# A decoder layer on one Trainium2 core: three groups of fp32 products as split products, base rows through DRAM

## What is computed

```
x = x + attn(layernorm(x))        # 16 heads of 128, window 128, rotary, q and k normed, a sink logit
x = x + cross(layernorm(x), ctx)  # 16 heads of 32, causal; out = concat(heads) @ Wout.T
x = x + ffn(layernorm(x))

attn:  q = h @ wq_comp @ wq_up    # 512 -> 128 -> 2048
       ... softmax ...            # then 2048 -> (4 groups) -> 512
ffn:   h = rmsnorm(x); base = x   # residual inside the sublayer as well
       routed = top 4 of 32 experts, w1: 512 -> 2*256, w2: 256 -> 512, silu(g)*u
       shared = silu(h @ sg) * (h @ su) @ sd      # 512 -> 512 -> 512
       out = base + routed + shared
```

## Time and profile before

| | |
|---|---|
| median of three runs | 1190.68 us |
| the profiled execution, its own time | 1187.81 us |
| its span, first to last instruction | 1185.9 us |
| mean granted TensorE clock | 0.989 |
| TensorE (PE) busy | 1141.3 us, 96% |
| weight loads (PEld) | 901.9 us, 76% |
| VectorE (DVE) | 811.3 us, 68% |
| ScalarE (ACT) | 594.3 us, 50% |
| GpSimd (POOL) | 344.8 us, 29% |

### The profile page before, as it was taken

One profiled execution on the slowest core, in us unless ns is written; L12 is line 12 of the kernel. 1 busy time (PEld: TensorE's weight loads), 2 busy tenths in 40 slices (PEclk: granted clock), 3 DMA queues, 4 the chain that ended last, 5 costly groups with the idle time before them and its releaser, 6 DMA issues. The chain is left out here.

```text
span 1185.9 us, 21051 instructions
## 1 busy us (share of the span) xinstructions
PE 1141.3 (96%) x7761; PEld 901.9 (76%) x7762; DVE 811.3 (68%) x1392; ACT 594.3 (50%) x1404; POOL 344.8 (29%) x279
## 2 busy tenths in 40 slices
PE   6989999999999999999999989999999999999995
PEld 3457677777767777776777666887889999999994
DVE  1255797889789878978987886643266666666662
ACT  1334554565455446545544644421146666666662
POOL 0011103211311221131123112222046666666643
PEclk9999999999999999999999989999999999999998
DMA  8450000000000000000000005042089999999974
GB/s 279 143 175 19 1 9 10 14 16 2 16 14 9 9 14 16 8 10 14 9 9 16 14 10 204 9 163 80 28 293 264 258 261 280 269 274 271 271 148 54
DMA packets 62598, 117.59 MB, mean 99 GB/s; under 512 B 10932, under 2 KB 14564, under 8 KB 62388
## 3 DMA queue, kind: packets, MB, share of 16 engines
q1 hardware_dynamic: 44820, 82.46, 20.6%
q0 software_dynamic: 17728, 34.44, 14.6%
HBM read 93.55 MB, written 28.13 MB: 103 GB/s over the span
## 5 line engine op out<-in xcount | busy, mean ns | idle before, releaser
L1503 POOL TENSOR_TENSOR rall<-qkv_var,phalf 100x17 f32<-100x17 f32 x16 | 49.1, 3071 | 404.4 <-DVE qkv_var L1177 404.4
L391 PE MATMUL QS<-xh,wh 128*128 128x256 f32 x512 | 147.2, 288 | 0.0
L392 PE MATMUL QS<-xl,wh 128*128 128x256 f32 x512 | 144.8, 283 | 0.0
L393 PE MATMUL QS<-xh,wl 128*128 128x256 f32 x512 | 144.8, 283 | 0.0
L1581 POOL DMA_INDIRECT out_rows<-work,idx x64 | 106.1, 1658 | 101.3 <-DMA out_rows<-work,idx 47.1
L391 PE MATMUL W<-wch,oth 128*100 128x512 f32 x256 | 105.1, 410 | 0.0
L392 PE MATMUL W<-wcl,oth 128*100 128x512 f32 x256 | 100.6, 393 | 0.0
L393 PE MATMUL W<-wch,otl 128*100 128x512 f32 x256 | 100.4, 392 | 0.0
L392 PEld LDWEIGHTS QS<-xl,wh 128*128 128x128 f32 x512 | 98.2, 192 | 1.2
L391 PEld LDWEIGHTS QS<-xh,wh 128*128 128x128 f32 x512 | 98.0, 191 | 1.2
L393 PEld LDWEIGHTS QS<-xh,wl 128*128 128x128 f32 x512 | 98.1, 192 | 0.0
(11 more groups left out here) (225 smaller groups left out, 2863.3 us busy)
## 6 DMA issues: line engine op xcount, KB each, us to landing
raw<-in_w SPq DMA_DIRECT2D x24, 1024.0 KB
raw<-in_w SPq DMA_DIRECT2D x24, 512.0 KB
work<-in_w SPq DMA_DIRECT2D x8, 1024.0 KB
work<-in_w SPq DMA_DIRECT2D x8, 512.0 KB
hx_rows<-h3x SPq DMA_DIRECT2D x16, 212.5 KB
h_columns<-h3s SPq DMA_DIRECT2D x16, 200.0 KB, 1.9
h3T<-h_columns SPq DMA_DIRECT2D x4, 800.0 KB, 15.2
out_rows<-ytiles POOLq DMA_DIRECT2D x14, 200.0 KB, 2.5
```

Source lines behind the costliest of these rows:

```text
L391: mm(dst, ah, bh, start=start, stop=False)
L392: mm(dst, ah, bl, start=False, stop=False)
L393: return mm(dst, al, bh, start=False, stop=stop)
L1503: return nc.gpsimd.tensor_tensor(out=dst, in0=src, in1=phalf[:, 0:src.shape[1]], op=ALU.pow)
```

## The change

1. `queries` for sequences 2 to 15 and `cross_out` for all become split products. The weights are split once: ScalarE copies `w_uph` and `w_outh` in step 0, VectorE subtracts `w_upl` at the end of step 0 and `w_outl` in step 1. Per step ScalarE's copy of the compressed query now writes the high part `hqh`, and VectorE gets `queries_low` (128 x 100); ScalarE's copy of the cross values writes `oxh`, and VectorE gets `values_low` (128 x 400).
2. To make room, `resid` holds eight sequences' rows instead of sixteen. After the third norm SP stores the base rows of a sequence to DRAM (`row_out`) and in steps 2 to 9 loads the residual rows of the sequence eight later into the place (`row_in`). Before the shared network's sums it loads all base rows back (`base_back`), in tiles of 128 tokens.
3. The shared network's second layer goes over 13 tiles: three of 128 tokens in each group of 400, and one of the 16 tokens left in each of the four groups. ScalarE and VectorE copy and subtract these 16 columns apart (`lfh`, `lfl`) for each inner product.
4. `cross_out` in the loop writes QS's bank 3 instead of W's. TensorE's heads 12 and 13 of `project` move behind `cross_transposed`, head 14 behind `cross_values`; on VectorE `rotate_keys` moves behind `rotate`; on ScalarE the exponential of the router moves behind the copies of the cross probabilities. Some semaphores are merged.

```
+HELD = 8
+LEFT = QW % BLK
+WHOLE = 2
             def queries(c):
+                whole = isinstance(c, int) and c < WHOLE
                 pe.wait_ge(s.hqT, c + 1)
+                if not whole:
+                    pe.wait_ge(s.hq_low, c - WHOLE + 1)
+                    if isinstance(c, int) and c == WHOLE:
+                        pe.wait_ge(s.low, NH + 1)
                 for i in range(4):
-                    mm(qb[i][0:T, :], hqT[:, :], w_up[:, 512 * i:512 * (i + 1)], start=True, stop=True).then_inc(s.q_ps, 1)
+                    w = slice(512 * i, 512 * (i + 1))
+                    if whole:
+                        last = mm(qb[i][0:T, :], hqT[:, :], w_up[:, w], start=True, stop=True)
+                    else:
+                        last = split_product(qb[i][0:T, :], hqh[:, :], hql[:, :], w_uph[:, w], w_upl[:, w], True, True)
+                    last.then_inc(s.q_ps, 1)
...
-            def cross_out(b):
+            def cross_out(b, bank):
-                pe.wait_ge(s.oxT, b)
+                pe.wait_ge(s.ox_low, b)
...
                 for k in range(KC):
-                    last = mm(wb[3][0:T, :], oxT[:, T * k:T * (k + 1)], w_out[:, 512 * k:512 * (k + 1)],
-                              start=k == 0, stop=k == KC - 1)
+                    c, w = slice(T * k, T * (k + 1)), slice(512 * k, 512 * (k + 1))
+                    last = split_product(bank[0:T, :], oxh[:, c], oxl[:, c], w_outh[:, w], w_outl[:, w], k == 0, k == KC - 1)
...
             def row_out(c):   # SP
+                sp.wait_ge(s.ln3_base, c + 1)
+                sp.wait_ge(s.row_st, 48 + 16 * c)
+                sp.dma_start(dst, resid[0:T, slot]).then_inc(s.row_st, 16)
+            def row_in(c):
+                sp.wait_ge(s.row_st, 48 + 16 * (c + 1))
+                sp.wait_ge(s.ld_x, 16 * (c + 1))
+                sp.dma_start(rv[:, bass.ds(c, 1), :], xv[:, bass.ds(c + HELD, 1), :]).then_inc(s.ld_x, 16)
...
             sp.wait_ge(s.x2_ps, NB)
+            sp.wait_ge(s.ld_x, 16 * (HELD + 1))
+            sp.wait_ge(s.row_st, 48 + 16 * NB)
+            for g in range(4):
+                base_back(g)
+            for g in range(4):
+                at = QW * g + 3 * BLK
+                sp.dma_start(back_left[LEFT * g:LEFT * (g + 1), :], based[at:at + LEFT, :]).then_inc(s.ld_x, 16)
...
+            def queries_low(c):   # VectorE
+                dve.wait_ge(s.hqT, c + 1)
+                dve.wait_ge(s.q_ps, 4 * c)
+                tt(hql[:, :], wb[1][:, 0:T], hqh[:, :].bitcast(fp32), ALU.subtract).then_inc(s.hq_low, 1)
+            def values_low(b):
+                dve.wait_ge(s.oxT, b)
+                dve.wait_ge(s.x2_ps, b - 1)
+                tt(oxl[:, :], wb[1][:, 0:QW], oxh[:, :].bitcast(fp32), ALU.subtract).then_inc(s.ox_low, 1)
...
-            def shared_rows(g, some=range(4)):
+            def shared_rows(g, some=range(3)):
                 for t in some:
+                    u = 3 * g + t
+                    dve.wait_ge(s.sh_y_ps, u + 1)
+                    if 2 <= u <= 10:
+                        dve.wait_ge((s.sh_st0, s.sh_st1)[u % 2], 16 * (u // 2))
+                    if t == 0:
+                        dve.wait_ge(s.ld_x, 16 * (HELD + 9))
+                    tt(ytile[sum_at(u)], back[g][:, HID * t:HID * (t + 1)], wb[t][:, :], ALU.add).then_inc(s.sh_y, 1)
```

More of the change, by code:

```diff
@@ L324, in step @@
                     sp.dma_start(dst, h3x[:, :]).then_inc(s.hx_st, 16)
-            pipeline(sp, step)
+                if do.C:
+                    row_out(b - 2)
+                if swap:
+                    row_in(b - 2)
+            step(0)
+            step(1)
+            with sp.Fori(2, HELD + 2) as b:
+                step(b, True)
+            again[0] = 1
+            with sp.Fori(HELD + 2, NB - 1) as b:
+                step(b)
+            step(NB - 1)
             def load_columns(g, done):
@@ L607, in step @@
                     router(b - 2)
-                if do.A:
-                    project(b, range(12, 14))
                 if do.X:
@@ L617, in step @@
                 if do.A:
-                    project(b, range(14, 15))
+                    project(b, range(12, 14))
                 if do.X:
@@ L624, in step @@
                 if do.A:
-                    project(b, range(15, 16)).then_inc(s.x1_ps, 1)
+                    project(b, range(14, 16)).then_inc(s.x1_ps, 1)
                 if do.C:
                     if do.X:
-                        pe.wait_ge(s.oxT, b)
+                        pe.wait_ge(s.ox_low, b)
                     ranks(b - 2)
                 if do.X:
-                    cross_out(b)
+                    pe.wait_ge(s.pxT, 4 * b)
+                    cross_out(b, qb[3])
             join(range(0, 8))
@@ L730, in _ @@
             shared_outer(3)
+            left_outer()
             def inner(e, v):
@@ L824, in compressed @@
                 act.wait_ge(s.q_ps, 4 * c)
-                copy(hqT[:, :], banks[1][:, 0:T]).then_inc(s.hqT, 1)
+                whole = isinstance(c, int) and c < WHOLE
+                copy((hqT if whole else hqh)[:, :], banks[1][:, 0:T]).then_inc(s.hqT, 1)
                 act.wait_ge(s.kv_ps, c + 1)
@@ L1277, in step @@
                 if do.Q:
-                    if isinstance(b, int) and b < 2:
-                        dve.wait_ge(s.ld_x, 16 * (b + 1))
+                    if isinstance(b, int) and b == 0:
+                        dve.wait_ge(s.ld_x, 16)
+                    elif not isinstance(b, int) or b >= HELD - 1:
+                        dve.wait_ge(s.ld_x, 16 * (b + 1 - HELD) + 32 if again[0] or isinstance(b, int) else 16)
                     ln_stats(0, b + 1, s.ln1_stats, s.ln1_var)
@@ L1325, in step @@
                     rotate(b + 1)
+                if do.Q:
+                    rotate_keys(b + 1)
                 if do.X:
                     cross_normed(b)
+                if isinstance(b, int) and b == 1:
+                    out_weights_low()
                 if do.Q:
@@ L1362, in _ @@
             joined(range(13, 14))
-            pipeline(dve, step)
+            step(0)
+            step(1)
+            with dve.Fori(2, HELD - 1) as b:
+                step(b)
+            for b in range(HELD - 1, HELD + 2):
+                step(b)
+            again[0] = 1
+            with dve.Fori(HELD + 2, NB - 1) as b:
+                step(b)
+            step(NB - 1)
             def split_low(n):
```

206 lines of the change are left out of this document (132 added, 74 removed).

## The result

| | before | changed |
|---|---|---|
| median of 20 runs each, us | 1193.95 (1186.55 to 1211.33) | 1189.16 (1180.54 to 1203.72) |
| ratio, 95% interval | 1 | 0.9955 (0.9934 to 0.9975) |
| span of the profiled execution, us | 1185.9 | 1181.5 |
| granted clock | 0.989 | 0.984 |

The ratio leaves out the executions that took over 1.5% longer than the fastest of their kernel. By it the change gains 5.4 us, 0.45%; forecast were 13.9 and a median of 1176.8 us. Of the 12.4 us between that and the measured median, 3.3 are the kernel before itself: its median was 1190.68 us over the first three runs and is 1193.95 over 20. The two profiles differ by 4.4 us, and that difference is read stretch by stretch.

What follows compares the result with a forecast made beforehand. TensorE was taken to fill the 41.40 us step, VectorE's chain close behind. Loop -9.8, step 15 -0.8 and shared network -3.3 gave -13.9 from 1187.81: 1173.9, plus 2.9 for the median, 1176.8 us; range 1167 to 1188.

Steps and rivals of the forecast that it cites:

- Split products: TensorE's `queries` and `cross_out`: four split products take 2.80 us, saving 0.63 and 0.69, 1.32 us a step.
- The wait at `hql`: TensorE in front of `queries`: 0.78 us of the saving turns into waiting for VectorE's subtraction, taken as 0.25 us.
- The ring: Loop steps: TensorE and VectorE wait on each other, so a step goes from 41.40 to 40.65 us, gaining 0.75.
- Rival 1: Loop: TensorE keeps the bound and a step gives all 1.6 us; 11 us more gain, 1166 us; chance 0.10.
- rival 2: Loop: VectorE's added work costs 0.75 us more a step, so the loop gives 0; 1186.6 us; chance 0.24.
- Step 15: Last step: step 14's `cross_out` saving passes through, with the wait of `cross_values`: -0.8 us, bounds 0 to -1.0.
- Group 0: Shared network's first group: base rows and a store delay product 7 to about 804.8; +2.3 us, bounds 0 to +10.
- rival 4: Loop: the wait in front of `queries` lowers the clock each step, 22 us on top, 1199 us; chance 0.05.
- Rival 3: Shared network: base rows land 12 us later at half the load rate, 1189 us; chance 0.07.
- The experts: Experts' stretch behind the shared network: its own 300 us untouched, 0 forecast.

Runs made afterwards that it cites:

- e4: Changed kernel with `queries` plain in all steps, `cross_out` still split: median 1188.65 us, ratio 0.9962, step 40.76 us.
- e8: Changed kernel with `cross_out` plain, `queries` still split: 1203.71 us, measured once, step 40.81 us.
- e9: Changed kernel with `queries` and `cross_out` both plain, the moves kept: 1193.78 us, measured once, step 41.20 us.
- e3: Changed kernel with SP loading the experts' weights only when the third sum is made: 1183.61 us, measured once.
- e11: Kernel before, with VectorE's shared_low(6) and shared_inner(7) ahead of shared_rows(0): median 1190.79 us, ratio 0.9973.
- e2: Changed kernel with the first group's base rows read back during step 15, first sums waiting for these alone: median 1178.35 us, ratio 0.9889.
- e10: Changed kernel: rotate_keys behind values_low, first base rows early, experts' weights behind third sum, product 7 and index columns ahead of sums; median 1168.71 us, ratio 0.9798.
- e12: Changed kernel with first base rows read early, product 7 ahead of the first sums, index columns ahead of the second group's: 1176.21 us, measured once.
- e1: Changed kernel with VectorE's shared_low(6) and shared_inner(7) ahead of shared_rows(0): median 1182.97 us, ratio 0.9916.
- e6: Changed kernel with `rotate_keys` moved behind `values_low`: 1199.02 us, measured once, step 40.56 us.
- e7: Changed kernel with `rotate_keys` behind `values_low`, and `hqh` copied and `hql` made earlier: median 1189.86 us, ratio 0.9983, step 40.71 us.

## Why the prediction was wrong, and where it was right

- **Split products.** 0.70 us each, 2.80 a set: right. The wait at `hql`, 0.78 forecast, measured 0.71; `hql` itself 0.25, as forecast. The Trainium skill's 215.7 ns from start to start (TensorE: Matmul & The Clock Gate, "Wait — 56ns, not 53.3ns?") would be 2.59 us a set; the trace has 2.80, or 233 ns a product, at a granted clock of 1.00.
- **The ring.** Right. A step of 40.65 was forecast and 40.77 measured; e4, e8 and e9 show that VectorE's chain caps the gain. That the 13 steps together came within 0.5 us of the forecast is partly luck: 0.63 a step were 8.2 us, and 1.1 came from steps that I had not looked at one by one. Rival 1 (TensorE keeps the bound, 39.8) and rival 2 (41.4) are out. I had called the unhindered saving 1.32 us; the splits' real worth in this loop is 0.43, and the moves' 0.20.
- **Step 15.** From its first transpose to its residual addition 37.72 us instead of 38.38: -0.7, forecast -0.8. But behind it 0.5 us were lost again up to the first outer product, where I had nothing; a new wait of 1.42 us of TensorE for ScalarE's `qpT` stands there. Ahead of `qpT` ScalarE copies `w_sgh`, which waits 2.66 us for its loads where it had waited 1.15. This was not tested apart.
- **Group 0: the step that failed.** The prediction said "product 7 is made at about 804.8 instead of 802.46. That is +2.3 us", with bounds of 0 to +10. It was +8.3, and with the half clock behind the long wait +9.5. The mechanism was right, base rows, store, product 7 in one chain; three durations in it were too small (the store that SP waits for, the loads, the store of the first sum), and the clock behind the wait was put at nothing. The wait at inner product 9, for which the prediction had "near 7 us" and at most 10, was 12.97. "Issue to landing of such a store takes 2.64 us" came from a row where the queues were about to run empty; here the same store took 5.6 us beside the experts' weights, which e3 turned back to 2.5. The rows I had nearly right: from the first issue to the first sum's start 15.4 us instead of 14.2 (785.8 to 800.0); but the issue came 1.5 us late, since SP goes on only 3.7 us behind the issue of the last base row's store (774.65 to 778.38), where I had put a landing of 1.9. I wrote that what the loads push back has 60 us of time; the question was what pushes them.
- **The clock.** I had priced a clock drop in the loop (rival 4), where it did not happen, and not at the long wait, where it did.
- **Rival 3**, the rows late by 12 us at half the rate, was the nearest to what came, with another cause: the rate was 331 to 360 GB/s in these windows, above the 259 I used, but the experts' weights took a part of it.
- **The experts.** 1.3 us more over 32 experts, where I had nothing. Nearly all of it is the clock in the last outer product. Up to its start the stretch takes 288.22 us before and 288.41 now. Its four starts on the line of high*high then span 2.18 us before (granted clock 1.00 from 1170 to 1174) and 3.29 us now (0.59 from 1167 to 1171), both behind a wait of 2.32 us. In e11, the kernel before with one edit, they span 2.80 us, so part of this differs between executions.

## What to carry to other kernels

When two engines close a ring, shortening one side is worth only the distance to the other, and here either of two edits alone was worth as much as both; find every crossing of the two chains before adding up two edits. A duration from issue to landing is a number of the place it was read at: price it again with what will run beside it after the change. And in an in-order engine, put what the bottleneck waits for ahead of what waits for DMA: that move, made at both places and with the first rows read early, left no wait for the base rows. But measure it against the old kernel too: there the profile shows 3.8 us of its gain as well.

## What the hardware showed

The store of the first sums landed in 2.5 us in e3 and in 5.6 to 6.4 us beside loads at a DMA share of about 1.0 (the change and e2); it was 2.5 us again in e10, where the experts' loads come later, and 6.5 us in e12, where they do not. The Trainium skill (DMA: Bandwidth & Descriptors, "Latency and other measured facts") says that access to HBM takes 0.2 us on average and 2 us at high load, and that a lighter load means a smaller fixed cost. The direction agrees; the 3 to 4 us more that these rows show are beyond it. TensorE's granted clock was 0.57 and 0.58 in the two windows around a wait of 13 us, and 1.00 throughout a loop with waits of 0.7 us in every step. Behind like waits the clock fell in some executions and not in others. The keys of step 2 stood at 146.29 us in the change and at 152.55 in e1, whose edit lies 600 us later. In both TensorE idles over 3 us in front of step 0's keys (3.31 and 3.12) and 2.43 in front of step 1's; the windows behind the first of these waits, in the change and in e1:

```profile
70.00:80.00 10.00, 10.00 (x60) 6.80 (x58) 7.17 (x10) 2.89 (x6) 0.56 (x1) 1.00 0.15 57
70.00:80.00 10.00, 10.00 (x59) 8.47 (x58) 4.17 (x6) 2.41 (x6) 0.56 (x1) 0.73 0.16 58
```

Behind the second wait, from 110 to 120, the clock is 1.00 in the change and 0.69 in e1. By an estimate from these windows, 10 x (0.27 + 0.31) = 5.8 us, the clock is nearly all of the difference of 6.3. The experts' stretch took 300.1 and 301.0 us in e6 and e7, against 291.7 in the change, with TensorE waiting 0.9 to 2.1 us for gathered rows at five and six experts; nothing in their edits reaches there. By their single totals (1199.02 and 1203.71 us) e6 and e8 would have looked slower than the change, although the loop of e6 is faster and a steady step of e8 is within 0.04 us of it.
